# Loading x in natural order, one home per mixed tile, and a shorter routing chain, in an AdaLN mixture-of-experts kernel

## The reference, cut to what matters

```python
agg_w = jnp.einsum('bk,koi->boi', att, weight[..., 0]); agg_b = att @ bias_k
xt = (jnp.einsum('boi,bih->boh', agg_w, x) + agg_b[:, :, None]).reshape(-1, 512)
scores = softmax(xt @ router_w + router_b) + router_bias
# best 2 of 4 groups of 4 experts (by their maximum), then the best 2 experts of these
h = silu(xt @ w1 + b1) * (xt @ w2 + b2)             # per expert, 512 -> 128
y = sum over the two experts of score * (h @ w3 + b3)
z = silu(xt @ sw1 + sb1) * (xt @ sw2 + sb2) @ sw3 + sb3   # shared, 512 -> 256
out = x + y + z
```

## Time and profile before

| | us |
|---|---|
| median of three runs | 256.04 |
| the profiled execution | 257.06 |
| its span | 255.3 |
| TensorE busy | 231.4 |
| VectorE busy | 130.2 |
| expert loop begins | 99.38 |

### The profile page before, as it was taken

One profiled execution on the slowest core, in us unless ns is written; L12 is line 12 of the kernel. 1 busy time (PEld: TensorE's weight loads), 2 busy tenths in 40 slices (PEclk: granted clock), 3 DMA queues, 4 the chain that ended last, 5 costly groups with the idle time before them and its releaser, 6 DMA issues.

```text
span 255.3 us, 4083 instructions
## 1 busy us (share of the span) xinstructions
PE 231.4 (91%) x1179; PEld 151.0 (59%) x1180; DVE 130.2 (51%) x273; ACT 77.0 (30%) x173; POOL 107.5 (42%) x127
## 2 busy tenths in 40 slices
PE   7875078899999989999999999999999999999994
PEld 7741044468875346667777777777776754444441
DVE  0372043558999978433343333333324321079995
ACT  3351063503147200333333333343433332100220
POOL 5088035640030245456666666666466331000080
PEclk9957556999999999999999999999999999999999
DMA  6999994899997937965545544355454221999974
GB/s 204 200 224 224 310 365 149 302 352 399 425 403 286 425 143 227 352 205 164 167 164 164 164 128 160 140 171 171 134 188 143 93 93 66 336 387 387 395 303 164
DMA packets 22091, 60.50 MB, mean 237 GB/s; under 512 B 2645, under 2 KB 2901, under 8 KB 21820
## 3 DMA queue, kind: packets, MB, share of 16 engines
q1 hardware_dynamic: 16476, 42.48, 48.5%
q0 software_dynamic: 5600, 17.83, 21.1%
HBM read 43.52 MB, written 17.30 MB: 238 GB/s over the span
## 4 chain that ended last, share of the span: by engine, by line
PE 71%; DVE 14%; issue 7%; DMA 5%; ACT 2%; DVEq 1%; POOL 0%; SPq 0%; POOLq 0%; ACTq 0%
PE psum L552 59%; PE psum L721 6%; PE psum L628 4%; DVE x_early L1211 4%; DMA wexp<-expert_rows 3%; DVE xT L1211 2%; PE psum L734 2%; ACT xt_sb L829 2%; DVE xT L947 1%; DVE xt_sb L1211 1%; DMA expert_rows<-late_region,to_slot 1%; DVE x_early L947 1%; DVE xT L987 1%; DVE r L1167 1%; DVE xt_sb L947 1%
## 5 line engine op out<-in xcount | busy, mean ns | idle before, releaser
L552 PE MATMUL psum<-wexp,r 128*128 x272 | 68.5, 381 | 0.4 <-DVE r L1167 0.2
L552 PEld LDWEIGHTS psum<-wexp,r 128*128 128x128 f32 x272 | 48.5, 190 | 22.9 <-issue 16.8
L947 DVE TENSOR_TENSOR r<-psum,ebias 128x256 f32<-128x256 f32 x34 | 14.4, 425 | 65.2 <-PE psum L552 64.1
L493 POOL DMA_INDIRECT expert_rows<-late_region,to_row x33 | 33.4, 1011 | 33.5 <-ACT late_region L890 24.7
L487 POOL DMA_INDIRECT late_region<-xt_rows,from_row x36 | 35.3, 980 | 17.9 <-issue 10.0
L552 PE MATMUL psum<-wexp,xt_sb 128*128 x68 | 34.8, 594 | 0.0
L552 PE MATMUL psum<-xT,shared_sb 128*128 128x512 f32 x64 | 28.0, 593 | 0.0
L884 ACT ACTIVATE r<-r 128x128 f32<-128x128 f32 x34 | 10.6, 311 | 56.2 <-DVE r L947 51.6
L628 PE MATMUL psum<-ident,xt_sb 128*128 128x128 f32 x64 | 13.3, 356 | 14.2 <-ACT xt_sb L829 14.1
L890 ACT ACTIVATE late_region<-psum 128x512 f32<-128x512 f32 x34 | 20.3, 598 | 15.3 <-issue 9.6
L1167 DVE COPY r<-psum 128x512 f32<-128x512 f32 x36 | 24.5, 681 | 0.2 <-PE psum L721 0.2
(11 more groups left out here) (177 smaller groups left out, 266.9 us busy)
## 6 DMA issues: line engine op xcount, KB each, us to landing
wexp<-expert_pack SPq DMA_DIRECT2D x16, 768.0 KB, 8.7
wexp<-expert_rows SPq DMA_DIRECT2D x8, 1024.0 KB, 13.8
xt_rows<-xt_sb SPq DMA_DIRECT2D x16, 256.0 KB, 2.6
x_early<-x SPq DMA_DIRECT2D x8, 256.0 KB, 8.5
late_region<-x SPq DMA_DIRECT2D x8, 256.0 KB, 14.4
x_early<-x SPq DMA_DIRECT2D x2, 1024.0 KB, 13.9
ebias<-expert_bias SPq DMA_DIRECT2D x1, 2048.0 KB, 19.1
out_dram<-x_early SPq DMA_DIRECT2D x8, 256.0 KB, 8.8
```

Source lines behind the costliest of these rows:

```text
L493: nc.gpsimd.indirect_dma_start(out=y_dram[:, :], out_offset=bass.IndirectOffsetOnAxis(ap=rows_of.bitcast(U32), axis=0), in_=y_sb[:, slot, ...
L552: return nc.tensor.matmul(dst, lhsT, rhs, start=start, stop=stop)
L947: return nc.vector.tensor_tensor(dst, a, b, op)
```

## The change

x is loaded in natural order, one transfer per group over all 128 partitions, so `x_tile(4g+q)` holds batch rows 16g+4q to 16g+4q+3. Mixed tile 4g+r now holds rows 4q+r of the group. The copy of the transpose into `xT` puts the columns back in natural order, and the store of a mixed tile writes four blocks of 32 rows to DRAM. Tiles 0 to 3 stay in `xt_sb`; tiles 4 to 15 each get room in the places 12 to 15 of `wexp`, which are loaded only when the three tiles on each are stored and transposed. Since x keeps its order, the second load of 2 MB of x (L366) goes. The router's bias is added in the copy of the chunk logits. VectorE and ScalarE each copy half of the mixing matrices. ScalarE adds the bias for a whole group before it splits the group before it. In the routing, 16 matmuls give counts over all tiles, 16 more add the counts of earlier tiles to the positions; both choices' positions come from one multiply and one reduce; a group's penalty is one addition. The counts stand in the middle of `shared_up(1, 0)`, the gates' transposes in the middle of `shared_up(1, 1)`, and tile 4 of `shared_down` behind the dispatch.

```diff
+        XT_HOMES = ((0, GT),) + tuple((GT + 3 * n, GT + 3 * n + 3) for n in range((NT - GT) // 3))
+        XT_PLACE = E - (NT - GT) // 3
+        def xt_tile(t):
+            return xt_sb[:, t * DIM:(t + 1) * DIM] if t < GT else \
+                wexp_flat[:, XT_PLACE * EW + (t - GT) * DIM:XT_PLACE * EW + (t - GT + 1) * DIM]
...
-                for r in range(BPT):
-                    first = (g * BPT + r) * BPT
-                    sp.dma_start(dst[r * IN_C:(r + 1) * IN_C], x[first:first + BPT].rearrange("q i d -> i q d")
-                                 ).then_inc(x_loaded[g], 16)
+                sp.dma_start(dst, group_of_x(g)).then_inc(x_loaded[g], 16)
...
-                sp.dma_start(xt_dram[t * P:(t + 1) * P, :], xt_ring[:, t % RING, :]
-                             ).then_inc(xt_stored[t % RING], 16)
+                g, r = divmod(t, GT)
+                sp.dma_start(xt_dram[g * GN:(g + 1) * GN, :].rearrange("(q r o) d -> r q o d", q=BPT, r=BPT)[r],
+                             xt_tile(t)).then_inc(xt_stored[home_of(t)], 16)
...
+            def load_over_xt(h):
+                first, end = XT_HOMES[h]
+                place = XT_PLACE + h - 1
+                sp.wait_ge(xt_stored[h], 16 * (end - first))
+                sp.wait_ge(xtT_done, end)
                 sp.dma_start(wexp[:, place, :], expert_pack[place]).then_inc(half_loaded[0], 16)
-            for g in range(EARLY):
-                sp.dma_start(x_early[:, g * GT:(g + 1) * GT, :], group_of_x(g)).then_inc(x_natural_loaded, 16)
+            for h in (1, 2, 3):
+                load_over_xt(h)
             sp.wait_ge(b3_ready, 1)
             sp.dma_start(ebias_flat, expert_bias.to_broadcast([P, E * 2 * INTER])).then_inc(half_loaded[0], 16)
+            load_over_xt(4)
...
-                if s % GT == 1 and s > GT:
+                if s % GT == 0 and s > 0:
                     chunk_logits(s // GT - 1)
...
+            def ranked():
+                pe.wait_ge(chosen_ready, 1)
+                for t in range(NT):
+                    last = mm(psum[:, 4, 0:E], ones_bf[:, :], chosen[:, t * E:(t + 1) * E],
+                              start=(t == 0), stop=(t == NT - 1))
+                last.then_inc(counts_done, 1)
+                mm(psum[:, 5, 0:NT * E], before[:, :], chosen, stop=False)
+                for t in range(NT - 1):
+                    last = mm(psum[:, 5, (t + 1) * E:NT * E]..., ones_bf[:, :], chosen[:, t * E:(t + 1) * E]...)
+            shared_up(1, 0, between={(0, C - 1): ranked})
+            shared_up(1, 1, between={(0, C - 1): gates_transposed})
             shared_down(0)
-            shared_down(1, [0])
...
-            for t in range(NT):
-                act.wait_ge(xt_done, t + 1)
-                if t >= RING:
-                    act.wait_ge(xt_stored[t % RING], 16 * (t // RING))
-                    act.wait_ge(xtT_done, t - RING + 1)
+            for g in range(NG):
+                for t in range(g * GT, (g + 1) * GT):
+                    act.wait_ge(xt_done, t + 1)
+                    nc.scalar.activation(xt_tile(t), psum[:, t % GT, :], ACT.Identity,
+                                         bias=mix_bias[:, t:t + 1]).then_inc(xt_ready, 1)
...
-                if t % 2 == 1 and 1 < t < GT * 2 + 2:
-                    if t == 3:
+                if t % 2 == 1 and GT <= t < NT - GT:
+                    if t == GT + 1:
                         dve.wait_ge(shared_loaded, 16)
```

More of the change, by code:

```diff
@@ L456, in _ @@
             W = EARLY * GT
-            for u in (0, 1, W, 2, W + 1, 3, W + 2, W + 3, *range(GT, W)):
+            for u in (0, W, 1, W + 1, 2, 3, W + 2, W + 3, *range(GT, W)):
                 pool.wait_ge(*((part_ready, u + 1) if u < W else (w_part_ready, u - W + 1)))
@@ L479, in _ @@
             pool.wait_ge(tables_ready, 1)
+            for h, (first, end) in enumerate(XT_HOMES):
+                pool.wait_ge(xt_stored[h], 16 * (end - first))
             def hold(semaphore, value):
@@ L673, in shared_down @@
                     mm(bank, gateT[:, t * P:(t + 1) * P], eb3x, start=False, stop=True).then_inc(down_done, 1)
[L675 to L684, removed]
+            def ranked():
[6 more added lines that the diff above has]
+                for t in range(NT - 1):
+                    last = mm(psum[:, 5, (t + 1) * E:NT * E].rearrange("p (t e) -> p t e", e=E), ones_bf[:, :],
+                              chosen[:, t * E:(t + 1) * E].unsqueeze(1).to_broadcast([P, NT - 1 - t, E]),
+                              start=False, stop=(t == NT - 2))
+                last.then_inc(ranks_done, 1)
             def gates_transposed():
@@ L710, in _ @@
             last.then_inc(dispatch_done, 1)
-            shared_down(1, range(1, GT - 1))
+            shared_down(1, range(GT - 1))
             pe.wait_ge(tables_ready, 1)
@@ L816, in _ @@
             act.wait_ge(pe_cond, 5)
-            for r in range(BPT):
-                rows = slice(r * IN_C, (r + 1) * IN_C)
-                nc.scalar.activation(mix_bias[rows, :], mixes_bias[rows, r], ACT.Copy).then_inc(bias_copied, 1)
+            for q in range(BPT):
+                rows = slice(q * IN_C, (q + 1) * IN_C)
+                nc.scalar.activation(mix_bias_of[rows], mixes_bias[rows, q], ACT.Copy).then_inc(bias_copied, 1)
             for g in range(NG):
-                copy_mixes(lambda dst, src: nc.scalar.activation(dst, src, ACT.Copy), g, BPT - 1
-                           ).then_inc(mix_copied_too, 1)
+                for r in range(BPT // 2, BPT):
+                    last = copy_mixes(lambda dst, src: nc.scalar.activation(dst, src, ACT.Copy), g, r)
+                last.then_inc(mix_copied_too, 1)
             act.wait_ge(bias_copied, BPT)
-            for t in range(NT):
-                act.wait_ge(xt_done, t + 1)
-                if t >= RING:
-                    act.wait_ge(xt_stored[t % RING], 16 * (t // RING))
-                    act.wait_ge(xtT_done, t - RING + 1)
[L829 to L836, removed]
+            for g in range(NG):
[3 more added lines that the diff above has]
+                                         bias=mix_bias[:, t:t + 1]).then_inc(xt_ready, 1)
+                if 1 <= g <= EARLY:
+                    act.wait_ge(xT_ready, g * GT)
+                    for u in range((g - 1) * GT, g * GT):
+                        whole, part, _ = split_of(u)
+                        nc.scalar.activation(part, whole, ACT.Copy).then_inc(part_ready, 1)
             act.wait_ge(shifted_ready, 1)
@@ L846, in _ @@
             act.wait_ge(router_loaded, 16)
-            act.wait_ge(xtT_done, NT)
-            for r in range(RING):
-                act.wait_ge(xt_stored[r], 16 * (NT // RING))
+            act.wait_ge(xtT_done, GT)
+            act.wait_ge(xt_stored[0], 16 * GT)
             shared_silu(0)
-            shared_silu(1, [0])
             act.wait_ge(gates_ready, 1)
@@ L966, in _ @@
             for g in range(NG):
-                for r in range(BPT - 1):
+                for r in range(BPT // 2):
                     last = copy_mixes(V.tensor_copy, g, r)
```

102 lines of the change are left out of this document (49 added, 53 removed).

## The result

The change made the kernel slower: 263.93 us (median of 4 runs, 263.7 to 264.0) against 255.31 us (median of 4, 254.47 to 256.28) on the same chip, a ratio of 1.034 [1.029, 1.038]. The forecast was 265 (255 to 271), slower at 0.75. The profiled execution took 263.92 us, its span 262.2; the sum for it was 266.2. The stores' new order explains all of the loss: with everything else kept and the tiles stored as they lie, the kernel takes 238.06 us, a ratio of 0.932 [0.929, 0.936] to the kernel before. The median of the kernel with quarters leaves out one execution of 250.32 us, which was in the chip's slower state.

The account below looks back on a forecast made before the run. It took the mixing stage, waiting on loads and stores, as the loose place of a mostly busy TensorE. Profiled 257.06 + 5.1 (later loop) + 4.0 (low clock) = 266.2, so 265 for a median; range 255 to 271.

Parts of the forecast that it names:

- The likeliest case: Mixed-tile stores on four engines delay expert weights, so the loop starts 5.1 us later; slower, chance 0.72 of 0.80.
- Loads: Start-up and mixing: x at 387 GB/s instead of 226, `shared_pack` near 20.5, shared expert at 36.6, 16.7 us earlier.
- Routing: Routing up to the expert loop: TensorE ready 0.4 us earlier, bounds 1.2 earlier to 0.8 later.
- The term for the small matmuls: Routing on TensorE: the 32 small matmuls cost about 2.0 us instead of 0.25.
- Stores: Mixed-tile stores: 2.77 us each, sixteen 44.3 us; last place lands at 104.5, loop starts 5.1 us later than 99.38.
- The 4: DMA spread of each mixed-tile store: a DRAM-side outer count of 4 puts it on 4 engines, not 16.
- the same four: DMA engines of the stores: all sixteen stores use the same four engines each time, which no row showed.
- The forecast's low end, 256: Whole kernel: 256 us if four engines run at 26.6 GB/s for small rows, 7 us sooner, with a short low clock.
- the sign given: Store queue: stores landing later and later, 10 to over 30 us after issue instead of 2.6, would show the forecast right.
- Clock: Expert loop's start: TensorE begins at 1.2 GHz after standing 20 us, costing 4.0 us (full price 4.7).
- Even stores: Rival for the mixed-tile stores: spread evenly over engines, last place near 78, time 240.0 or 239 median; chance 0.16.
- Slow x with even stores: Rival for x's load: no faster, VectorE waits at tile 5 until 31.8, 247 us; slow x 0.04, faster 0.01.

Follow-up runs that it names:

- the kernel with quarters: Changed kernel with each mixed tile stored by four transfers of 32 partitions, each to 32 rows in a row: 246.84 us, 0.966 of the kernel before.
- even stores: Changed kernel with each mixed tile stored as it lies and the gather's row numbers swapped by five small VectorE operations: 238.06 us, 0.932 of before.
- the old routing: The kernel with even stores, with the routing part of the change undone: 240.3 us, 0.941 of the kernel before.
- the two-block kernel: Changed kernel with each mixed tile stored by two transfers of 64 partitions, each to two blocks of 32 rows in DRAM: 305.99 us in one run.

## Why the prediction was right

The likeliest case came true, by its own mechanism: the outer count of 4, four engines that are the same each time, and weights that land behind their stores. That the sum came within 2.3 us of the profiled 263.92 is in part luck, for several terms were off with both signs. Step by step:

**Loads.** `shared_pack` was to land at 20.5. It was issued at 6.28 and its landing took 17.8 us, so it landed near 24, 3.6 late: the queue moved 216 to 277 GB/s in most of its first 6 us, not the 387 that was taken for all of them. It cost nothing in the mixing, for ScalarE no longer waits for the queue. The mixing began at 12.92 before and the forecast had it no later; it came at 14.48. ScalarE's eight copies of mixing matrices don't lie beside the work but hold the first matmul: TensorE waits 1.77 us for them, where it waited 1.28 for VectorE. The other 1.1 us vary from one execution to the next (13.17 with even stores, 14.59 with the old routing). The clock rose at the beginning of group 1 (0.84 in the stretch from 20 to 24 us), and 4.96 a group was a little less than the 5.2 of the forecast. So errors of both signs gave 36.54 for the shared expert against 36.6, which is luck in part.

**Routing.** 0.4 us earlier was forecast, bounds −0.8 to +1.2. The runs show 1.6, outside the bounds. The term for the small matmuls was too dear: all 32 took 52.18 to 53.57, 1.4 us instead of 2.0, and 16 of them with 16 columns only 0.56, 35 ns each, while the row that the price was taken from has 96 columns. The other part is the gather: it is hidden fully, and what is saved is the 1.69 us that the old-routing kernel waits, where 0.93 was counted. 0.4 + 0.6 + 0.8 is 1.8, near the 1.6.

**Stores.** The 4 held, and so did "the same four". The price of one store didn't: 2.55 us at 103 GB/s, not 2.77, so the sixteen took 41 us and not 44.3. That took back about what the late `shared_pack` had added. The last place landed at 102.9 where 104.5 was forecast, and the loop then began 2.0 us after the landing, for which the sum had nothing: so 104.90 came out near 104.5 by terms that cancel. The 1 us from the last packet to the semaphore stands in no row of this case. The forecast's low end, 256, was too low for its own conditions. Both nearly came true (26 GB/s for an engine with small rows too, and a short low clock), and the time was still 264: the low end gave the rate 7 us, and the stores gained 3.5.

What the forecast didn't see is where the wait is spent. It let the weights be issued on time and queue beneath the stores on four engines. In fact SyncE itself was held at every store, so from 28 to 60 us the twelve other engines got only two places' weights (issued at 33.99 and 46.32). By the share, which is nowhere below that of four busy engines from 24 us to 104, both should give the same end; no run tests that. The stores' landing shows the difference: 10 to over 30 us after issue was the sign given, and the last one, whose issue was itself held back, landed after 13.45. The gathers were late too (8.5 us to landing, against 3.7 with even stores), so that TensorE was ready at 87 rather than 82.3; that was hidden behind the weights.

**Clock.** 4.0 us forecast, 1.4 measured against the profiled execution before (2.1 against even stores). This was the term with the largest error by proportion. It was taken from the mixing stage, where the low clock lasted 9.4 us with many small waits in between the earlier trace rows. In the dense loop it was back at 1.00 in the stretch from 110, that is after at most 5 us. With the measured terms the sum is 257.06 + 5.5 + 1.4 = 264.0, against 263.92; that closes the account and tests nothing.

**Rivals.** Even stores was priced at 240.0 for a profiled execution; built, it took 237.99. Of the 2.0 us, 1.1 lie before the loop (81.20 against 82.3): the routing gave 1.2 more than forecast and the shared expert began 0.5 earlier, less what the five small operations took. 0.9 lie behind the loop's start, where the profiled execution before was slow (155.9). Slow x with even stores was priced at 247; built, it took 247.95. Both prices were good. What decided between the cases was the outer count, which the earlier trace rows suggested for equal sides; that the smaller side decides and that the engines stay the same was an assumption there, and the two-block kernel bears it out.

What isn't settled: how much work the queue takes before it holds its issuer. The runs show that stores of 256 KB on four engines do and stores with 64 KB on four engines don't, and no run went between.

## What to carry to other kernels

Before a transfer's view is rearranged, look at the outer count of both sides: a view that looks free for its unchanged rows of 2 KB can leave 4 of 16 engines, and most of the price falls on what stands behind it in the queue. When a permutation must be paid somewhere, pay it in row numbers that are computed anyway (five small operations) rather than in the access pattern of 16 large stores. And follow a gain up to the point where the next resource is late: 16.8 us were really gained here, and none was left at the loop.

## What the runs showed of the hardware

- With an outer count of 4, transfers ran at a share of 0.26 to 0.28 and 103 to 108 GB/s, with four small packets each; with 2, at 0.13 and 51 to 52, with two each; with 128, at 1.06 and 419. Each time that is about 26 GB/s for an engine. The Trainium skill ("DMA: Bandwidth & Descriptors", the section on why a DMA increments its semaphore by 16) gives the rule; the number of engines agrees in all three. That the engines are the same ones each time is borne out by 305.99 us; which ones they are no run shows.
- A queue with much work in it stops its issuer: 2.46 us per store on SyncE, against 0.32 to 0.5 where the engines keep up. Whatever the issuer has to send next is held too, though other engines are free. It isn't a matter of few engines alone: eight places that go over all 16 took 11.70 us to issue (69.90 to 81.6 us in the changed kernel).
- Issuing itself has a price: 0.53 us for each of 64 small stores, 34 us of SyncE in all. Stores in four quarters were 8.8 us slower than whole tiles (246.84 against 238.06), through this and, as the rates suggest, through the lower rate of 32 partitions.
